# Dense products of a graph-network kernel over 136 instead of 144 columns, on one Trainium2 core

## The chip, the cores and the metric

The kernel runs on one core of one Trainium2 chip (trn2). The metric is device time in microseconds (us) of one execution. A profiled execution gives the trace from which all rows here come. Engines are called PE (TensorE), DVE (VectorE), ACT (ScalarE), POOL (GpSimd) and SP (SyncE, which here only issues transfers).

## What is computed

A graph network of two layers over 6250 nodes and 100000 edges, 128 features each, then a residual sum and a layer norm. The edges are sorted by their target `dst`.

```python
def _layer(h, edge_feats, src, dst, deg, iso, Wn, Ws, Wi, num_nodes):
    msg = (h[src] + edge_feats) @ Wn.T
    agg = jax.ops.segment_sum(msg, dst, num_segments=num_nodes)
    agg = agg / jnp.maximum(deg, 1.0)[:, None]
    self_msg = jnp.where(iso[:, None], h @ Wi.T, h @ Ws.T)
    x = agg + self_msg
    return jnp.where(x >= 0, x, RRELU_SLOPE * x)
...
    h = _layer(x, edge_feats, src, dst, deg, iso, Wn0, Ws0, Wi0, num_nodes)
    h = _layer(h, edge_feats, src, dst, deg, iso, Wn1, Ws1, Wi1, num_nodes)
...
x = _layernorm(x + h)
```

## The kernel before, in words

**Chunks, windows, groups.** 128 edges are a chunk, four chunks a window, four windows a group of 2048 edges. There are 782 real chunks, 196 windows and 49 groups (0 to 48). Since edges are sorted by target, the targets of a window fit in `W` = 40 consecutive columns of `sums`, and those of a group in `SPAN` = 144. The work runs in beats, one window to a beat as a rule.

**Two ways to sum the rows of h.** The way of the windows: POOL gathers, for each chunk, the 128 source rows by an indirect DMA (`gather`, line 511; each row is three bf16 parts of an f32 value), and PE multiplies them by a one-hot matrix of 40 columns into a `ps_win` bank (`sum_chunk`, line 1190), which DVE adds to `sums` (`add_window`, line 731). There are `ROWS` = 5 window slots for gathered rows, so POOL may be at most five gathered windows ahead: it waits on `window_summed`. The dense way: for a group that is kept, DVE makes two one-hot matrices per chunk (`make_codes`, lines 714 to 720), PE multiplies them into a count matrix (`count_piece`, lines 1239 and 1243), ACT writes it from PSUM to `counts` (`keep_chunk`, line 1044). A kept group then has, for each of 49 tiles of 128 nodes, a block of 128 x 144 counts, and `multiply` (line 1251) computes `h_parts` times `counts`: 49 tiles x 3 parts = 147 matmuls of 144 columns a group, all into one PSUM bank. `take_dense` (line 753) adds the bank to 144 columns of `sums`.

**Layer 0.** 31 groups are counted and stored to HBM (`store_counts`); 20 of them (`USED`) are also multiplied by PE in this layer, bank `ps_dense`, in pieces of five or six tiles a beat between the window's matmuls and the count pieces, as `plan_layer0` lays them out. The other groups' rows are gathered: 442 gathers from `x_parts_rows`, after 20 early ones. As a rule two windows of three are gathered; in four steps (with groups 7, 19, 31, 43) one of three. Each trio of 384 nodes whose sums are complete passes through the node stages; its new rows go to `h_parts_rows`.

**Layer 1.** All 31 kept groups are multiplied (`multiply_kept`), their counts loaded back by SP in 217 cuts of seven tiles, 21 cuts ahead. The 18 others (72 windows, 286 gathers from `h_parts_rows`) are gathered. PE does a few cuts and then one window in each beat; the node stages of a trio (lines 1303 and 1316) follow when its sums are complete.

**Setup.** DVE tests in the setup that the input fits the layout (line 616 on), collects the differences side by side in `wrong`, takes their largest (line 636), and the flag `general` made of it (line 681) sends the engines into the fast program or into a slow general one. PE, ACT and POOL start their main work behind that flag.

Of the kernel before, what the change touches and what calls it, by code (L numbers as in the profile page):

```python
# [46 lines left out]
def gnn_resnorm_kernel(nc, x_rows, x_cols, src, dst, edges, wn0, ws0, wi0, wn1, ws1, wi1, out):  # L47
    f32, i32 = mybir.dt.float32, mybir.dt.int32
    bf16, f16 = mybir.dt.bfloat16, mybir.dt.float16
    ALU, ACT, AX = mybir.AluOpType, mybir.ActivationFunctionType, mybir.AxisListType  # L50
# [13 lines left out]
    GC = 16  # L64
    GW = GC // SUB
    GROUPS = CHUNKS // GC
    STEPS = GROUPS // 3
    W = 40
    CW = 13
    UP = 7  # L70
    SPAN = 144
    CLEAN = 24
    PARTS = 3
    CUT = 7
# [5 lines left out]
    BANKS = 3  # L80
# [6 lines left out]
    assert GROUPS == 3 * STEPS + 1 and TRIOS == STEPS + 1 and TILES % CUT == 0  # L87
    assert COLS == TRIOS * TRIO and CHUNKS % GENERAL == 0 and N + P + SPAN <= COLS

# [7 lines left out]
    USED = sorted([g for g in KEPT if g % 3 == 0] + [7, 19, 31, 43])  # L97
# [55 lines left out]
    h_parts_rows = nc.dram_tensor("h_parts_rows", (P + TILES * P, PARTS * D), bf16, kind="Internal").ap()  # L153
    counts_kept = nc.dram_tensor("counts_kept", (len(KEEPABLE), P, TILES * SPAN), bf16, kind="Internal").ap()

# [3 lines left out]
    with ctx:  # L159
        def sb(name, shape, dt=f32):  # L160
            return ctx.enter_context(nc.sbuf_tensor(name, shape, dt))

        def sem(name):
            return ctx.enter_context(nc.semaphore(name))

        SUM, DEG = range(2)
        sums = sb("sums", [P, 2, COLS])
        h_parts = sb("h_parts", [P, TILES, PARTS, D], bf16)
        counts = sb("counts", [P, BUFFERS, TILES, SPAN], bf16)

# [59 lines left out]
        def bank(name, n=1):  # L230
            return ctx.enter_context(nc.psum_tensor(name, [P, n, 512], f32))

        ps_win = [bank(f"ps_win{i}") for i in range(2)]
        ps_count = bank("ps_count", BANKS)
        ps_dense = bank("ps_dense")
# [8 lines left out]
        setup_step = sem("setup_step")  # L244
# [78 lines left out]
        def at(v, n=1):  # L323
            return bass.ds(v, n)
# [16 lines left out]
        def steps(t):  # L341

            return t[:, :].rearrange("p (s c) -> p s c", c=2 * GC)
# [14 lines left out]
        def dense_bank(nth):  # L358

            if nth < len(USED):  # L360
                return ps_dense[:, 0, 0:SPAN]
            return ps_count[:, (nth - len(USED)) % BANKS, 0:SPAN]

        def real(u):

# [11 lines left out]
        def _(sp):  # L377
# [59 lines left out]
            def load_counts(q):  # L437
# [6 lines left out]
                if q >= BUFFERS * CUTS:  # L444
                    sp.wait_ge(cut_multiplied, q - BUFFERS * CUTS + 1)
                t = slice(CUT * cut, CUT * (cut + 1))
                sp.dma_start(counts[:, i % BUFFERS, t, :].rearrange("p t s -> p (t s)"),
                             counts_kept[FIRST_COL[KEPT[i]] // GC, :, CUT * cut * SPAN:CUT * (cut + 1) * SPAN]
                             ).then_inc(counts_loaded[q % (BUFFERS * CUTS)], 16)
# [105 lines left out]
        def _(dve):  # L555
            def setup(ins):
                ins.then_inc(setup_step, 1)
                done[0] += 1
                return done[0]
# [16 lines left out]
            bases = dst_f[0:1, :]  # L576
# [10 lines left out]
            for i in range(CUTS + 1):  # L587
                if i < CUTS:
                    t = slice(CUT * i, CUT * (i + 1))
# [3 lines left out]
                if i:  # L593
                    t = slice(CUT * (i - 1), CUT * i)
# [5 lines left out]
            grouped = bases[:, 0:3 * STEPS * GC].rearrange("p (g c) -> p g c", c=GC)  # L600
# [5 lines left out]
            n = setup(nc.vector.tensor_tensor(stride, bases[:, 1:3 * STEPS * GC + 1], bases[:, 0:3 * STEPS * GC],  # L606
                                              ALU.subtract))
# [3 lines left out]
            def part(count):  # L611
                place[0] += count
                return wrong[:, place[0] - count:place[0]]
# [7 lines left out]
            last = by_group[:, :, GC - 1]  # L621
            setup(nc.vector.tensor_scalar(part(3 * STEPS), last, float(CW - SPAN), None, ALU.add))
            setup(nc.vector.tensor_scalar(part(3 * STEPS), last, -1.0, float(SPAN - CLEAN - CW), ALU.mult, ALU.add))
            firsts = bases.rearrange("p (k c) -> p k c", c=SUB)[:, :, 0]
            ahead = part(WINDOWS)
            n = setup(nc.vector.tensor_tensor(ahead[:, 0:WINDOWS - 1], firsts[:, 1:WINDOWS], firsts[:, 0:WINDOWS - 1],
                                              ALU.subtract))
            n = setup(nc.vector.tensor_scalar(ahead[:, WINDOWS - 1:WINDOWS], firsts[:, WINDOWS - 1:WINDOWS],
                                              -1.0, float(N), ALU.mult, ALU.add))
# [3 lines left out]
            n = setup(nc.vector.tensor_tensor(part(GROUPS), first_dst[:, :],  # L633
                                              bases.rearrange("p (g c) -> p g c", c=GC)[:, :, 0], ALU.subtract))
# [6 lines left out]
            for b in range(2):  # L641
                c = slice(HALF * b, HALF * (b + 1))
# [7 lines left out]
            n = setup(nc.vector.tensor_tensor(below[:, HALF:], dst_f[:, HALF - 1:CHUNKS - 1], ps_count[:, 1, 0:HALF],  # L650
                                              ALU.subtract))
            dve.wait_ge(setup_step, n)
            n = setup(nc.vector.reduce_max(bad[:, 0:1], below[:, 1:], AX.X))
            n = setup(nc.vector.tensor_reduce(rel_w[:, 0:1], above, AX.X, ALU.min))
            dve.wait_ge(setup_step, n)
            n = setup(nc.vector.scalar_tensor_tensor(bad[:, 0:1], rel_w[:, 0:1], -1.0, bad[:, 0:1], ALU.mult, ALU.max))
            dve.wait_ge(setup_step, n)
            n = setup(nc.vector.tensor_tensor(bad[0:1, 0:1], bad[0:1, 0:1], bad[0:1, 1:2], ALU.max))
# [6 lines left out]
            n = setup(nc.vector.tensor_single_scalar(high, src_i, 7, ALU.logical_shift_right))  # L665
            dve.wait_ge(setup_step, n)
            setup(nc.vector.tensor_copy(steps(lane), of_kept(low)))
            n = setup(nc.vector.tensor_copy(tile_of, high))
# [6 lines left out]
            n = setup(nc.vector.scalar_tensor_tensor(steps(before)[:, :, 1:2 * GC], below_now[:, :, 1:2 * GC], float(-P),  # L675
                                                     tile_now[:, :, 0:2 * GC - 1], ALU.mult, ALU.add))
            n = setup(nc.vector.memset(steps(before)[:, :, 0:1], float(P)))
# [45 lines left out]
            def load_columns(table, first, count):  # L723
                return nc.values_load_multi_w_load_instructions(
                    table[0:1, first:first + count], (mybir.EngineType.DVE,), min_val=P, max_val=COLS - SPAN,
                    skip_runtime_bounds_check_because="the setup keeps the bases within the columns")[1]
# [18 lines left out]
            def take_dense(g, windows, added):  # L745

                col = load_columns(base_i, GW * g, 1)[0]
                if windows:
                    dve.wait_ge(window_added, windows)
                if added:  # L750
                    dve.wait_ge(dense_added, added)
                s = sums[:, SUM, at(col, SPAN)]
                nc.vector.tensor_tensor(s, s, dense_bank(added), ALU.add).then_inc(dense_added, 1)  # L753

            def node_inputs(layer, u):
# [243 lines left out]
        def _(act):  # L999
# [25 lines left out]
            def begin_job(j):  # L1025

                b = j % BUFFERS
                if j >= BUFFERS:
                    act.wait_ge(counts_stored[b], 16 * (j // BUFFERS))
                    if JOBS[j - BUFFERS] in USED:  # L1030
                        act.wait_ge(group_multiplied, USED_JOBS.index(j - BUFFERS) + 1)
                end = counts[:, b, :, SPAN - CLEAN:].bitcast(f32)
                nc.scalar.copy(end, zeros[:, 0:CLEAN // 2].unsqueeze(1).to_broadcast([P, TILES, CLEAN // 2]))

# [131 lines left out]
        def _(pe):  # L1166
# [80 lines left out]
            def multiply(b, bank, t0, t1):  # L1247

                for t in range(t0, t1):
                    for k in range(PARTS):  # L1250
                        last = nc.tensor.matmul(bank, h_parts[:, t, k, :], counts[:, b, t, :],  # L1251
                                                start=(t == 0 and k == 0), stop=(t == TILES - 1 and k == PARTS - 1))
                return last

            def multiply_counted(j, t):

                nth = USED_JOBS.index(j)
                if t == 0:
                    pe.wait_ge(piece_kept, 2 * GC * (j + 1))
                    if nth:  # L1260
                        pe.wait_ge(dense_added, nth)
                last = multiply(j % BUFFERS, dense_bank(nth), t, t + 1)
                if t == TILES - 1:
                    last.then_inc(group_multiplied, 1)

            def multiply_kept(q):

                i, cut = divmod(q, CUTS)
                nth = len(USED) + i
                pe.wait_ge(counts_loaded[q % (BUFFERS * CUTS)], 16 * (q // (BUFFERS * CUTS) + 1))  # L1270
                if i == 0:
                    pe.wait_ge(parts_loaded[cut], 16)
                if q == 0:
                    pe.wait_ge(piece_kept, 2 * GC * len(JOBS))
                if cut == 0 and i >= BANKS:
                    pe.wait_ge(dense_added, nth - BANKS + 1)
                multiply(i % BUFFERS, dense_bank(nth), CUT * cut, CUT * (cut + 1)).then_inc(cut_multiplied, 1)
# [184 lines left out]
```

## Time and profile before

| | |
|---|---|
| median of 3 runs | 1088.06 us (1087.48 to 1088.09) |
| the profiled execution, its own time | 1087.0 us |
| its span, first to last instruction | 1085.2 us |
| mean granted clock of TensorE | 0.963 |
| PE busy, share of the span | 954.0 us, 88% |
| POOL busy | 751.6 us, 69% |
| DVE busy | 692.2 us, 64% |
| ACT busy | 514.9 us, 47% |

Setup takes the first 38 us or so, layer 0 runs until about 680 us, a passage between the layers until 707 us, layer 1 from there on. Busy shares are of the whole span and hide that the two layers use the engines differently. Matmuls are pipelined: the duration of one says how long it is under way, and what it costs PE is the distance from its start to the next one's.

### The profile page before, as it was taken

The page shows a single profiled execution, that of the slowest core. Times are in us where ns is not written, and L with a number is a line of the kernel's source. Part 1 is how long each engine was busy: PE and PEld are TensorE (multiplying, and loading weights), DVE is VectorE, ACT ScalarE, POOL GpSimd, SP SyncE. Part 2 cuts the span into 40 slices and gives each one's busy share as a digit, 9 for nine tenths or more (in the row PEclk, how much of TensorE's full clock was granted, in tenths as well). Part 3 has the DMA queues.
Part 4 walks back from the last instruction along what each step waited for, and adds up shares of the span by engine and source line. Part 5 has one row for each costly group of instructions (what it writes and reads, how often), then busy time and mean ns, then how long its engine had stood idle before and what let it go on. Part 6 is the DMA issues. An engine that isn't in the chain of part 4 may idle for free.

```text
span 1085.2 us, 38525 instructions
## 1 busy us (share of the span) xinstructions
PE 954.0 (88%) x14592; PEld 894.2 (82%) x14592; DVE 692.2 (64%) x2386; ACT 514.9 (47%) x1143; POOL 751.6 (69%) x757
## 2 busy tenths in 40 slices
PE   1599999999999998998889987579999999999992
PEld 0489888888888887887878877479999999999991
DVE  8878987888897898887878875312334232423333
ACT  7477777777787787786767774100000000000000
POOL 8467756777767777767777547077777777777772
PEclk9999999999999999999999999589999999999995
DMA  9468878878888787787778768699988898889732
GB/s 306 154 199 275 287 224 277 274 256 274 276 269 276 242 307 248 254 300 257 232 247 283 241 213 306 218 366 312 278 272 269 266 283 264 266 268 286 230 103 69
DMA packets 154041, 277.50 MB, mean 256 GB/s; under 512 B 21458, under 2 KB 112572, under 8 KB 149884
## 3 DMA queue, kind: packets, MB, share of 16 engines
q1 hardware_dynamic: 93504, 184.10, 50.7%
q0 software_dynamic: 35584, 72.92, 23.1%
q10 hardware_dynamic: 24764, 17.95, 5.2%
q8 instruction: 120, 1.97, 0.7%
q14 instruction: 69, 0.57, 0.2%
HBM read 202.58 MB, written 72.30 MB: 253 GB/s over the span
## 4 chain that ended last, share of the span: by engine, by line
PE 46%; issue 5%; POOL 5%; DVE 3%; DMA 3%; ACT 2%; SPq 1%; ACTq 1%; DVEq 0%; POOLq 0%
PE ps_count L1251 24%; PE ps_win L1190 6%; PE ps_dense L1251 6%; POOL rows L511 5%; PE ps_count L1239 4%; PE ps_self L1303 3%; DMA rows<-x_parts_rows,idx 2%; PE ps_node L1316 2%; ACT counts L1044 1%; SPq L434 1%; DMA counts<-counts_kept 1%; DVE is_code L720 1%; DVE is_lane L718 1%; PE ps_win L1197 1%; PE ps_self L1285 1%
## 5 line engine op out<-in xcount | busy, mean ns | idle before, releaser
L511 POOL DMA_INDIRECT rows<-x_parts_rows,idx x442 | 445.8, 1008 | 197.1 <-issue 127.9
L1044 ACT CAST counts<-ps_count 128x294 f32 x992 | 437.7, 504 | 152.4 <-PE ps_count L1239 67.7
L511 POOL DMA_INDIRECT rows<-h_parts_rows,idx x286 | 275.7, 964 | 111.2 <-issue 81.7
L1239 PE MATMUL ps_count<-is_code,is_lane 128*128 128x294 bf16 x992 | 300.5, 309 | 34.4 <-ACT counts L1044 32.4
L1251 PE MATMUL ps_dense<-counts,h_parts 128*128 128x144 bf16 x2940 | 320.7, 227 | 3.4 <-DVE sums L753 3.3
L1251 PE MATMUL ps_count<-counts,h_parts 128*128 128x144 bf16 x4557 | 299.0, 227 | 10.3 <-DMA counts<-counts_kept 10.3
L1251 PEld LDWEIGHTS ps_count<-counts,h_parts 128*128 128x128 bf16 x4557 | 289.9, 98 | 11.1 <-DMA counts<-counts_kept 10.7
L1190 PE MATMUL ps_win<-onehot,feats 128*128 128x40 f32 (+1 forms) x1564 | 244.2, 235 | 20.3 <-DVE sums L731 12.2
L1251 PEld LDWEIGHTS ps_dense<-counts,h_parts 128*128 128x128 bf16 x2940 | 214.5, 98 | 39.0 <-ACT counts L1044 5.0
L1190 PEld LDWEIGHTS ps_win<-onehot,feats 128*128 128x128 f32 (+1 forms) x1564 | 206.7, 158 | 25.1 <-issue 15.7
L720 DVE TENSOR_SCALAR is_code<-codes,code 128x637 bf16<-128x637 f16 x496 | 196.8, 397 | 0.0
L731 DVE TENSOR_TENSOR sums<-sums,ps_win 128x80 f32 (+1 forms) x268 | 59.0, 220 | 182.1 <-PE ps_win L1190 130.2
L1056 ACT COPY self_sums<-ps_self 128x384 f32<-128x384 f32 (+1 forms) x34 | 16.1, 474 | 319.9 <-PE ps_self L1303 319.9
L1190 PE MATMUL ps_win<-onehot,rows 128*128 128x40 bf16 (+1 forms) x2224 | 149.0, 186 | 15.4 <-issue 10.6
L718 DVE TENSOR_SCALAR is_lane<-column,lane 128x128 bf16<-128x128 bf16 x496 | 135.8, 274 | 36.2 <-PE ps_count L1243 34.4
L1190 PEld LDWEIGHTS ps_win<-onehot,rows 128*128 128x128 bf16 (+1 forms) x2224 | 131.3, 112 | 17.1 <-issue 17.1
L1239 PEld LDWEIGHTS ps_count<-is_code,is_lane 128*128 128x128 bf16 x992 | 108.0, 110 | 44.6 <-ACT counts L1044 39.3
L1243 PE MATMUL ps_count<-is_before,is_lane 128*128 128x49 bf16 x465 | 88.5, 190 | 0.0
L690 DVE TENSOR_TENSOR onehot<-column,rel 128x160 f32<-128x160 bf16 x268 | 84.4, 317 | 1.7 <-issue 1.7
L705 DVE TENSOR_TENSOR feats<-feats_rest 128x512 bf16<-128x512 f32 x78 | 58.4, 749 | 2.7
L1190 PE MATMUL ps_win<-onehot,feats_rest 128*128 128x40 bf16 x310 | 56.0, 182 | 0.0
L703 DVE TENSOR_TENSOR feats_rest<-feats 128x512 f32<-128x512 f32 x78 | 53.1, 681 | 3.7 <-DMA feats<-in_edges_dram 3.7
(97 smaller groups left out, 784.2 us busy)
## 6 DMA issues: line engine op xcount, KB each, us to landing
counts_kept<-counts SPq DMA_DIRECT2D x31, 1764.0 KB
counts<-counts_kept SPq DMA_DIRECT2D x217, 252.0 KB, 4.1
feats<-in_edges_dram SPq DMA_DIRECT2D x196, 256.0 KB
rows<-x_parts_rows,idx POOLq DMA_INDIRECT x442
x_parts_rows<-h_parts SPq DMA_DIRECT2D x7, 672.0 KB
h_parts<-h_parts_rows SPq DMA_DIRECT2D x7, 672.0 KB, 9.4
h_parts_rows<-row_parts ACTq DMA_DIRECT2D x16, 288.0 KB
rows<-h_parts_rows,idx POOLq DMA_INDIRECT x286
```

The source lines that it names most:

```text
L511: nc.gpsimd.indirect_dma_start(rows[:, SUB * slot + c, :], None, table[:, :], bass.IndirectOffsetOnAxis(ap=indices[:, c:c + 1], axis=0)).t ...
L690: nc.vector.tensor_tensor(onehot[:, h:h + SUB, :], column[:, 0:W].unsqueeze(1).to_broadcast([P, SUB, W]), rel[:, chunk:chunk + SUB].unsque ...
L703: nc.vector.tensor_tensor(rest, f, upper(f), ALU.subtract).then_inc(feats_rest_made, 1)
L705: nc.vector.tensor_tensor(lower(f), rest, upper(rest), ALU.subtract).then_inc(feats_split, 1)
L718: nc.vector.tensor_scalar(is_lane[:, n % (AHEAD + 1), :], column[:, :], lane[:, col:col + 1], None, ALU.is_equal)
L720: nc.vector.tensor_scalar(is_code[:, n % AHEAD, :], codes[:, :], code[:, col:col + 1], None, ALU.is_equal).then_inc(codes_ready, 1)
L731: return nc.vector.tensor_tensor(s, s, p, ALU.add)
L1044: nc.scalar.copy(counts[:, j % BUFFERS, :, at(offset + first, count)], ps_count[:, q % BANKS, 0:count * TILES].rearrange("p (r t) -> p t r ...
L1190: last = nc.tensor.matmul(ps[:, 0, SUM * w:(SUM + 1) * w], left, right, start=first and i == 0, stop=final and i == len(lefts) - 1)
L1239: last = nc.tensor.matmul(ps[:, 0:count * TILES], is_lane[:, n % (AHEAD + 1), :], is_code[:, n % AHEAD, first * TILES:(first + count) * TI ...
L1243: last = nc.tensor.matmul(ps[:, 0:TILES], is_lane[:, (n - 1) % (AHEAD + 1), :], is_before[:, (n // 4) % 3, n % 4, :], start=False, stop=True)
L1251: last = nc.tensor.matmul(bank, h_parts[:, t, k, :], counts[:, b, t, :], start=(t == 0 and k == 0), stop=(t == TILES - 1 and k == PARTS - 1))
```

## The change

The products of kept groups take columns 0 to 135 of a count block, where they took all 144; their banks and the slice of `sums` that `take_dense` adds to are 136 wide. The blocks themselves, their storing and their loading stay 144 wide. In the setup one more test is made: from the first target of a group to that of the next it must be at most 135. No instruction changes its place in the order of its engine; DVE has two more, and the reduction at line 636 reads 48 more values.

```diff
     SPAN = 144
+    WIDE = 136
...
             if nth < len(USED):
-                return ps_dense[:, 0, 0:SPAN]
-            return ps_count[:, (nth - len(USED)) % BANKS, 0:SPAN]
+                return ps_dense[:, 0, 0:WIDE]
+            return ps_count[:, (nth - len(USED)) % BANKS, 0:WIDE]
...
+            reach = part(3 * STEPS)
+            n = setup(nc.vector.tensor_tensor(reach, bases.rearrange("p (g c) -> p g c", c=GC)[:, 1:3 * STEPS + 1, 0],
+                                              grouped[:, :, 0], ALU.subtract))
+            dve.wait_ge(setup_step, n)
+            setup(nc.vector.tensor_scalar(reach, reach, float(1 - WIDE), None, ALU.add))
...
-                s = sums[:, SUM, at(col, SPAN)]
+                s = sums[:, SUM, at(col, WIDE)]
                 nc.vector.tensor_tensor(s, s, dense_bank(added), ALU.add).then_inc(dense_added, 1)
...
-                        last = nc.tensor.matmul(bank, h_parts[:, t, k, :], counts[:, b, t, :],
+                        last = nc.tensor.matmul(bank, h_parts[:, t, k, :], counts[:, b, t, 0:WIDE],
```

## Rows read from the trace of the kernel before

**Rows 1.** The page, costliest groups: busy us, mean ns | idle before, releaser.

```profile
L511 POOL DMA_INDIRECT rows<-h_parts_rows,idx x286 | 275.7, 964 | 111.2 <-issue 81.7
L1251 PE MATMUL ps_dense<-counts,h_parts 128*128 128x144 bf16 x2940 | 320.7, 227 | 3.4 <-DVE sums L753 3.3
L1251 PE MATMUL ps_count<-counts,h_parts 128*128 128x144 bf16 x4557 | 299.0, 227 | 10.3 <-DMA counts<-counts_kept 10.3
```

**Rows 2.** Stretches: busy us (count) of PE, PEld, DVE, ACT, POOL; clock, DMA share, GB/s.

```profile
200.00:300.00 100.00, 93.32 (x1466) 85.16 (x1464) 86.28 (x301) 76.35 (x177) 76.83 (x77) 1.00 0.83 274
900.00:1000.00 100.00, 99.52 (x1661) 99.10 (x1659) 36.26 (x135) 3.14 (x9) 76.23 (x79) 1.00 0.90 271
```

**Rows 3.** POOL's waits, 700 to 1086 us: us in total, times, longest.

```profile
POOL rows L511 <- issue: 81.7, 268, 0.3
...
POOL rows L511 <- PE ps_win L1190: 5.2, 17, 0.3
```

**Rows 4.** POOL in order of time: start us, us; the last two begin and end layer 1.

```profile
171.59 1.09 POOL L511 DMA_INDIRECT rows<-x_parts_rows,idx  x1 [2.04 <-PE ps_win L1197]
...
327.93 0.94 POOL L511 DMA_INDIRECT rows<-x_parts_rows,idx  x1 [1.96 <-issue]
...
704.62 0.94 POOL L511 DMA_INDIRECT rows<-h_parts_rows,idx  x1 [24.39 <-DMA h_parts_rows<-row_parts]
...
1066.20 0.95 POOL L511 DMA_INDIRECT rows<-h_parts_rows,idx  x1 [0.30 <-issue]
```

**Rows 5.** The chain of waits in layer 1: start us, us, what.

```profile
707.39 5.63 PE ps_count L1251 x63
...
719.88 3.94 PE ps_count L1251 x63
723.83 0.56 issue
...
1058.70 3.43 DMA rows<-h_parts_rows,idx
```

**Rows 6.** The chain of waits in layer 0, 424 to 435 us: start us, us.

```profile
424.69 9.19 DMA rows<-x_parts_rows,idx
...
434.43 0.13 PE ps_count L1239
434.56 0.19 PE ps_dense L1251 x3
434.75 0.14 PE ps_win L1190 x6
```

**Rows 7.** PE's and POOL's longest waits in layer 0, from 60 us on.

```profile
PE ps_count L1239 <- ACT counts L1044: 31.3, 42, 1.9
...
POOL rows L511 <- PE ps_win L1197: 55.9, 38, 7.0
```

**Rows 8.** Line 1251 alone, 60 to 645 us: count, duration, first and last start.

```profile
L1251 PE MATMUL ps_dense<-counts,h_parts x2838: 222/224/328, 62.5 to 644.6; 128*128 128x144 bf16 x190
```

**Rows 9.** Shares of the chain of waits, in 500 to 560 and 560 to 645 us.

```profile
by line: PE ps_dense L1251 18.3%; issue 18.3%; PE ps_count L1239 13.5%; PE ps_win L1190 11.9%; DVE is_code L720 5.5%; DVE is_lane L718 3.9%; ACT counts L1044 2.5%; PE ps_self L1303 2.4%; DVE feats_rest L703 2.0%; DVEq L724 2.0%; DVE row_par
by line: PE ps_dense L1251 27.2%; PE ps_count L1239 20.7%; PE ps_win L1190 17.4%; ACT counts L1044 6.0%; issue 4.8%; PE ps_self L1303 3.3%; ACTq L1020 3.3%; PE ps_self L1285 2.7%; PE ps_win L1197 2.5%; PE ps_count L1243 1.8%; DVEq L724 1.6%
```

**Rows 10.** DVE in the setup, in order of time.

```profile
26.68 0.22 DVE L633 TENSOR_TENSOR counts<-first_dst,counts 1x49 f32<-1x49 f32 x1
26.93 1.56 DVE L636 TENSOR_REDUCE bad<-counts 1x1 f32<-1x1365 f32 x1
...
37.19 0.14 DVE L681 TENSOR_SCALAR general<-ps_node 1x1 int32<-1x1 f32 x1
```

**Rows 11.** Two stretches of lower granted clock (columns as in rows 2), and PE just before the first.

```profile
150.80:154.20 3.40, 3.40 (x36) 3.08 (x34) 2.33 (x11) 1.54 (x4) 0.00 (x0) 0.50 0.76 245
628.70:632.10 3.40, 3.40 (x38) 2.84 (x36) 2.99 (x10) 2.72 (x6) 2.26 (x3) 0.50 0.72 199
149.91 0.32 PE L1239 MATMUL ps_count<-is_code,is_lane 128*128 128x343 bf16 x1 [1.47 <-ACT counts L1044]
```

## The prediction

> **What bounds the kernel now.** I read the groups of instructions first, then busy time by stretches, then POOL's waits, then the chain of waits of each layer. In the groups the products on line 1251 are 7497 matmuls of 144 columns, 2940 in layer 0 and 4557 in layer 1, by far PE's largest item; that they last 227 ns each is their latency, not their cost [rows 1]. By stretches PE looks like the bound of both layers: 93% busy in layer 0 and 99.5% in layer 1 [rows 2]. The reader should not stop there. POOL is 76% busy in both, but a gather keeps it busy for 964 ns and is followed by a gap of 0.3 us [rows 1, 3]. In layer 1 all 285 gaps are of that kind: 268 put down to nothing, 17 to PE, and none, of either sort, longer than 0.3 us [rows 3]. POOL never stands still there. Its first gather starts at 704.62 and its last at 1066.20 us [rows 4]: 361.58 / 285 = 1.269 us for each. Layer 1 is thus as long as 286 gathers, and PE, nearly full, runs beside them. The chain says the same at both ends: at 723.83 us PE, having done 63 products, waits 0.56 us before its next window, and at the end the chain goes through a gather's landing at 1058.70 us [rows 5]. In layer 0 POOL does wait for PE, 55.9 us in all with one wait of 7.0 us, and PE waits for ACT, 31.3 us in 42 waits [rows 7]: PE is the usual bound, with interruptions.
>
> **The price of a column.** In the chain 63 products take 3.94 us, 62.5 ns each, and 3 take 0.19 us [rows 5, 6]. A window's 6 matmuls of 40 columns, with weight loads of the same size, take 0.14 us, 23 ns each, and a count piece of 294 columns 0.13 us [rows 6]. From 40 to 144 columns a column costs (62.5 - 23) / 104 = 0.38 ns, from 144 to 294 it costs (130 - 62.5) / 150 = 0.45 ns. These are the ends; I take 0.417 ns, one column per clock at the higher of the two levels (2.4 GHz), which lies between them. Eight columns are 3.3 ns a matmul (3.0 to 3.6).
>
> **PE's work.** Over both layers 7497 x 3.33 ns = 25.0 us of PE time go, 9.8 in layer 0 and 15.2 in layer 1.
>
> **Layer 1: nothing on the path.** The 15.2 us are hidden by POOL, whose 286 x 1.269 us do not depend on PE: it goes from release to gather with room to spare. PE will stand before its windows for rows, by 15.2 / 72 = 0.2 us a window, and be later for nothing. I take 0; a gain up to 15.2 us is the first rival.
>
> **Layer 0: about half.** Up to 645 us there are 2838 products [rows 8], 2838 x 3.33 ns = 9.5 us over 582 us. After that the chain is POOL's until the layers change, so the last 102 count for nothing. Two deductions. First, gathers bind here too, in places. In a step of twelve beats eight windows are gathered: 32 x 1.269 us = 40.6 us, while twelve beats of PE take 12 x 3.2 = 38.4 us (582 us over the 183 windows that lie there). Only the four steps with a fourth group, of 16 gathers, let POOL catch up. At the end of such a run the chain has a landing of 9.19 us at 424.69 us, after which PE goes on [rows 6]. From POOL's last long pause before it, of 1.96 us until 327.93 us [rows 4], to that landing's end at 433.9 us a faster PE only waits longer: 106 us, or 1.7 us of the 9.5. A run of the same make begins after a wait of 2.04 us at 171.59 us [rows 4] and should end at about 280; no wait of PE shows there, so I give it half, 0.9 us. That leaves 6.9. Second, ACT and DVE: line 1251 has 18.3% of the chain in 500 to 560 us, 11.0 us, and 27.2% in 560 to 645 us, 23.1 us [rows 9]. All its products there, at 2838 x 62.5 ns / 582 = 0.305 us a microsecond, would be 18.3 and 25.9 us. So 34.1 of 44.2 us, 77%, lie on the path. 6.9 x 0.77 = **5.3 us** gained. The ends are 2 us, if PE runs into ACT's evacuation each time, and 10.2 us, all 2838 at 3.6 ns.
>
> **Setup: 0.4 us lost.** DVE works without a pause from the tests to the flag at 37.19 us, and all main work is behind that. The new subtraction and the new addition, over 48 values each, have no row; the nearest is the subtraction over 49 values, 0.22 us, whose successor, which waits for it, starts 0.25 us after it [rows 10]. Two such steps cost at most 0.5 us, and 0.15 us if only their starts count; I take 0.35 us, and for the reduction 48 / 1365 x 1.56 = 0.05 us. Ends: 0.2 and 0.7 us. The addition on line 753 gets shorter by 8 columns, 51 times, beside PE's work: 0. Transfers keep their size: 0. The test itself holds for the reference's inputs: the largest of the 48 distances is 135, the last value allowed.
>
> **The sum.** -5.3 + 0.4 = -4.9 us. The profiled execution took 1087.0 us (its span 1085.2), so it would take 1082.1; the median of the runs is 1.1 us above it, and 1088.06 - 4.9 = **1083.2 us**.
>
> **Rivals.** *PE bounds layer 1 after all* (8%). For it: 99.5% busy. If the gathers got faster as PE takes less, both layers would gain: 9.5 x 0.77 + 15.2 - 0.4 = 22.1, 1066 us; half of it 1077. Against it: 285 gaps without one long wait.
>
> *Gathers and ACT swallow layer 0 too* (11%). If the run from 171 us on is fully bound and what PE gains goes into its 42 waits for ACT, 2 - 0.4 = 1.6 us are left: 1086.5 us, no change that can be told (a measurement of this kernel tells 0.2%, 2.2 us).
>
> *The change saves no PE time* (5%). Weight loads stay 128 columns, and a load is under way in 99.1 of 100 us [rows 2]. If a pair of load and product had a floor near 62 ns, 136 columns would cost the same, and 1088.5 us come out. Against it: pairs of 40 columns follow each other in 23 ns [rows 6], though only in sixes and twelves.
>
> The Trainium skill, "TensorE: Matmul & The Clock Gate", section Back-to-back issue gap, has the spacing in a stream of loads and matmuls set by both, with about 81 ns for 128 columns. By that rule this would be the outcome; but this trace has 62.5 ns for 144 columns in 63 of them, so its figure does not hold here [rows 5].
>
> *The clock falls more often* (6%, slower). Six stretches of 3.4 us in layer 0 have a granted clock of 0.50 (the 1.2 GHz level), the first at 150.80, the last at 628.70 us; just before the first PE had waited 1.47 us for ACT [rows 11]. Less work between equal waits makes PE's idle share larger. A stretch at the lower level costs 5.63 - 3.94 = 1.69 us, by the 63 products that start at 707.39 us against later ones [rows 5]. Six more would cost 10.1 us: 1088.1 - 4.9 + 10.1 = 1093.3 us. It decides from (4.9 + 2.2) / 1.69 = 4.2, so from five more. Against it: in 200 to 300 us, with 7% idle, the clock stays at 1.00 [rows 2].
>
> **How the numbers follow.** The forecast has 70%, and its cases with a gain over 2.2 us some 69; the rivals have 8, 11, 5 and 6. Faster by over 0.2%: 0.69 + 0.08 = 0.77. Within 0.2%: 0.01 + 0.11 + 0.05 = 0.17. Slower: 0.06. The range begins at 1078.3, the median less 10.2 us and with 0.4 us of setup, which leaves out most of the first rival, and ends at 1087.3, which takes in the second rival with the upper bound of the setup and leaves out the two others.
>
> **What would show it.** Right: products of 136 columns 59.2 ns apart in layer 1 (63 in 3.73 us); PE's busy share in 900 to 1000 us down from 99.5% to about 95%, with waits before line 1190; POOL's first and last gather of layer 1 still 361 to 363 us apart; POOL's first gather of layer 1 some 5 us earlier than 704.62; the flag 0.4 us later. Wrong: the distance between the first and last gather shrinks with PE's work (first rival); 63 products still take 3.94 us (third); more than nine stretches at the lower clock in layer 0 (fourth). If the first gather of layer 1 moves by less than 2 us, my share of layer 0 was too large; if by 9, the two deductions were wrong.

## The result

The change is faster by 0.36%: the ratio to the kernel before is 0.9964 with a 95% interval from 0.9951 to 0.9977. The medians of 20 runs each are 1085.21 us (1080.18 to 1087.57) and 1087.88 us (1083.88 to 1093.31). By the ratio that is 1087.88 x 0.0036 = 3.9 us (2.5 to 5.3), where 4.9 us were forecast.

Single executions of this kernel differ by several us, so one pair of profiles doesn't show the gain: the profiled execution after took 1087.57 us, with a span of 1085.8 us against 1085.2. What the profile does show is where time was freed and what stood in its place.

The page and its groups, the counterpart of [rows 1]. PE's busy time fell from 954.0 to 933.4 us:

```profile
PE 933.4 (86%) x14592; PEld 869.7 (80%) x14592; DVE 691.7 (64%) x2388; ACT 513.5 (47%) x1143; POOL 760.0 (70%) x757
...
L512 POOL DMA_INDIRECT rows<-h_parts_rows,idx x286 | 278.1, 972 | 111.9 <-issue 84.8
...
L1258 PE MATMUL ps_dense<-counts,h_parts 128*128 128x136 bf16 x2940 | 311.0, 224 | 3.9 <-DVE sums L760 2.2
L1258 PE MATMUL ps_count<-counts,h_parts 128*128 128x136 bf16 x4557 | 282.1, 223 | 10.0 <-DMA counts<-counts_kept 10.0
```

The chain of waits of layer 1 after (start us, us, what), as in [rows 5]: 63 products in 3.73 us, 59.2 ns each, where it was 3.94 us.

```profile
713.35 3.73 PE ps_count L1258 x63
718.30 3.73 PE ps_count L1258 x63
```

The same two stretches as in [rows 2], same columns. PE's share in layer 1 went from 99.52 to 94.46%, in layer 0 from 93.32 to 91.61%, and the DMA's in layer 1 from 0.90 to 0.88; DVE, ACT and POOL moved by half a point at most.

```profile
200.00:300.00 100.00, 91.61 (x1454) 83.29 (x1450) 86.28 (x303) 76.22 (x178) 76.83 (x77) 1.00 0.83 276
900.00:1000.00 100.00, 94.46 (x1636) 93.20 (x1634) 35.77 (x134) 3.14 (x9) 76.21 (x79) 1.00 0.88 270
```

Waits in 700 to 1086 us (us in total, times, longest): first PE before a window, before the change, then the same after it, then POOL after.

```profile
PE ps_win L1190 <- issue: 10.6, 9, 2.7
...
PE ps_win L1190 <- DMA rows<-h_parts_rows,idx: 4.7, 1, 4.7
```

```profile
PE ps_win L1197 <- issue: 29.6, 24, 3.9
```

```profile
POOL rows L512 <- issue: 84.8, 278, 0.3
POOL rows L512 <- DMA h_parts_rows<-row_parts: 25.0, 1, 25.0
POOL rows L512 <- PE ps_win L1197: 2.1, 7, 0.3
```

That is the story of layer 1. PE stood 10.6 + 4.7 = 15.3 us before its windows and now stands 29.6 us, 14.3 more for 15.2 us of work less, and POOL still has no gap over 0.3 us. A wait "for issue" is one for which the trace shows no releaser; before a window it is most likely for the landing of gathered rows. POOL's first and last gather of layer 1 after, against [rows 4]:

```profile
703.13 0.94 POOL L512 DMA_INDIRECT rows<-h_parts_rows,idx  x1 [25.02 <-DMA h_parts_rows<-row_parts]
...
1067.15 0.95 POOL L512 DMA_INDIRECT rows<-h_parts_rows,idx  x1 [0.30 <-issue]
```

They are 364.0 us apart, 1.277 us a gather, where it was 361.6 and 1.269. That is a little over the 361 to 363 us that I had named, and not for the 136 columns: the same distance is 361.7 us in a run with 136 columns in layer 1, and 364.4 us in the one with 144 there, 136 in layer 0 and half of that layer's gathers (both below).

The new test in the setup, DVE in order of time, against [rows 10]; the first fence is an earlier instruction in the trace before, whose counterpart begins the second:

```profile
24.88 0.41 DVE L618 TENSOR_SCALAR counts<-counts 1x512 f32<-1x512 f32 x1
```

```profile
25.40 0.41 DVE L619 TENSOR_SCALAR counts<-counts 1x512 f32<-1x512 f32 x1
...
26.29 0.22 DVE L627 TENSOR_TENSOR counts<-counts 1x48 f32<-1x48 f32 x1
26.55 0.18 DVE L630 TENSOR_SCALAR counts<-counts 1x48 f32<-1x48 f32 x1
26.65 0.50 DVE L633 TENSOR_TENSOR counts<-counts 1x195 f32<-1x195 f32 x1
...
27.68 1.61 DVE L643 TENSOR_REDUCE bad<-counts 1x1 f32<-1x1413 f32 x1
...
37.99 0.15 DVE L688 TENSOR_SCALAR general<-ps_node 1x1 int32<-1x1 f32 x1
```

From the start of the subtraction to that of the next old instruction it is 26.65 - 26.29 = 0.36 us, and the reduction takes 0.05 us more: 0.41 us. The flag itself came 0.80 us later than before (37.99 against 37.19), but 0.52 us of that was there before the first new instruction (25.40 against 24.88); from there to the flag it is 12.59 us against 12.31, 0.28 us more.

### The profile page after: what moved, and what is told of

The parts are those of the page before. It is cut to its first block, busy times and chain, and to the rows that moved or that the text cites. A ratio compares the mean times of both kernels' runs of the same rounds, so it can differ in the third digit from the quotient of the medians.

```text
span 1085.8 us, 38527 instructions
## 1 busy us (share of the span) xinstructions
PE 933.4 (86%) x14592; PEld 869.7 (80%) x14592; DVE 691.7 (64%) x2388; ACT 513.5 (47%) x1143; POOL 760.0 (70%) x757
## 4 chain that ended last, share of the span: by engine, by line
PE 48%; issue 6%; DVE 4%; DMA 3%; ACT 2%; POOL 2%; ACTq 1%; DVEq 0%; SPq 0%; POOLq 0%
PE ps_count L1258 25%; PE ps_win L1197 7%; PE ps_dense L1258 6%; PE ps_count L1246 5%; PE ps_self L1310 3%; PE ps_node L1323 2%; POOL rows L512 2%; DMA rows<-x_parts_rows,idx 1%; ACT counts L1051 1%; DVE is_code L727 1%; DMA counts<-counts_kept 1%; PE ps_win L1204 1%; DMA h_parts_rows<-row_parts 1%; DVE is_lane L725 1%; PE ps_self L1292 0%
## 5 line engine op out<-in xcount | busy, mean ns | idle before, releaser
L512 POOL DMA_INDIRECT rows<-x_parts_rows,idx x442 | 450.9, 1020 | 189.0 <-issue 127.9
L1258 PE MATMUL ps_dense<-counts,h_parts 128*128 128x136 bf16 x2940 | 311.0, 224 | 3.9 <-DVE sums L760 2.2
L1258 PE MATMUL ps_count<-counts,h_parts 128*128 128x136 bf16 x4557 | 282.1, 223 | 10.0 <-DMA counts<-counts_kept 10.0
L1258 PEld LDWEIGHTS ps_count<-counts,h_parts 128*128 128x128 bf16 x4557 | 273.5, 98 | 10.7 <-DMA counts<-counts_kept 10.4
L1258 PEld LDWEIGHTS ps_dense<-counts,h_parts 128*128 128x128 bf16 x2940 | 210.2, 98 | 39.7 <-ACT counts L1051 5.1
L1197 PEld LDWEIGHTS ps_win<-onehot,feats 128*128 128x128 f32 (+1 forms) x1564 | 205.9, 158 | 28.1 <-issue 19.9
L1197 PE MATMUL ps_win<-onehot,rows 128*128 128x40 bf16 (+1 forms) x2224 | 149.0, 186 | 32.4 <-issue 29.6
```

What stands on the lines that cost most here:

```text
L512: nc.gpsimd.indirect_dma_start(rows[:, SUB * slot + c, :], None, table[:, :], bass.IndirectOffsetOnAxis(ap=indices[:, c:c + 1], axis=0)).t ...
L1197: last = nc.tensor.matmul(ps[:, 0, SUM * w:(SUM + 1) * w], left, right, start=first and i == 0, stop=final and i == len(lefts) - 1)
```

## The experiments

The theory: layer 1 is as long as POOL's gathers, so what PE saves there is lost; in layer 0 PE bounds, but not everywhere, so about half counts. Rivals: PE's time counts alike in both layers; products don't get cheaper. Each ratio is to the kernel before, run beside it on the same chip, with its 95% interval; where us are given for a ratio, they are the ratio times 1088.

**One layer at a time.** The width of bank, slice and product is set by layer, `WIDE0` and `WIDE1`.

```diff
+    WIDE0, WIDE1 = 136, 144
...
-                        last = nc.tensor.matmul(bank, h_parts[:, t, k, :], counts[:, b, t, 0:WIDE],
+                        last = nc.tensor.matmul(bank, h_parts[:, t, k, :], counts[:, b, t, 0:bank.shape[-1]],
```

> 136 columns in layer 0 alone, 144 in layer 1, with the new test. Gathers bound layer 1 (my theory): all of the change's gain stands, 3.9 us (ratio 0.996). Rival, PE's time counts alike in both layers: 2940 of 7497 products, so 1.5 us (0.9986). Either way the first gather of layer 1 to the last takes 361 to 365 us.

> 136 columns in layer 1 alone, 144 in layer 0, with the new test. My theory: no gain, -0.5 to +1 us (1.000), products 59.2 ns apart, PE's busy share from 900 to 1000 us down to about 95% and gathers of layer 1 as before, 1.27 us each. Rival (PE counts in both layers): 2.4 us faster (0.9978).

Layer 0 alone: 0.9954 (0.9928 to 0.998), 5.0 us. Layer 1 alone: 1.0007 (0.9981 to 1.0032), nothing. The second run's POOL in order of time, and its stretch of 900 to 1000 us with the columns of [rows 2]:

```profile
710.57 0.94 POOL L513 DMA_INDIRECT rows<-h_parts_rows,idx  x1 [25.19 <-DMA h_parts_rows<-row_parts]
...
1072.29 0.94 POOL L513 DMA_INDIRECT rows<-h_parts_rows,idx  x1 [0.30 <-issue]
```

```profile
900.00:1000.00 100.00, 96.40 (x1674) 95.45 (x1672) 34.27 (x131) 3.14 (x9) 75.93 (x79) 1.00 0.87 268
```

361.7 us from first to last gather, within 0.2 us what it was, with PE relieved of 15 us. The whole gain is layer 0's. For the first run alone the rival's 1.5 us lie outside the interval of 2.2 to 7.8 us; for the second its 2.4 us lie just outside that of -3.5 to +2.1 (negative is slower), so the ratios of this pair alone lean to the theory and the trace settles it.

**A cut large enough to see.** `WIDE0, WIDE1 = 96, 96`: a product over 96 columns, columns 96 to 143 left out.

> Products and sums over 96 columns in both layers; leaves out the columns 96 to 143 of each group's product. A product should cost 96 x 0.417 + 2.5 = 42.5 ns, so that PE is relieved of 20 ns x 2940 = 59 us in layer 0 and 91 us in layer 1. My theory: layer 1 keeps its length (first to last gather 361 to 365 us) and layer 0 gives back 15 to 35 us, until gathers and ACT bind: 1053 to 1073 us. Rival (PE bounds layer 1): about 960 us. Third (a floor for a pair of weight load and product near 60 ns): 1084 us.

0.9865 (0.9806 to 0.9923), 14.7 us of 150 us of PE time, from a median of 1073.26 us. Its chain of waits, a stretch of layer 1, and POOL's first and last gather there:

```profile
726.78 2.68 PE ps_count L1259 x63
```

```profile
900.00:1000.00 100.00, 79.09 (x1622) 77.46 (x1619) 34.05 (x125) 2.93 (x8) 75.92 (x80) 0.93 0.86 269
```

```profile
685.83 0.95 POOL L513 DMA_INDIRECT rows<-h_parts_rows,idx  x1 [23.91 <-DMA h_parts_rows<-row_parts]
...
1049.45 0.95 POOL L513 DMA_INDIRECT rows<-h_parts_rows,idx  x1 [0.30 <-issue]
```

2.68 / 63 = 42.5 ns, as 96 x 0.417 + 2.5 gives: no floor for a pair of load and product down to there. PE is 79% busy in layer 1, and the gathers still take 363.6 us. Layer 0 gave back less than expected: 14.7 us, just under the 15 to 35. In this execution the granted clock also fell more often in layer 0: 47.8 us at 0.50 up to 650 us, where it was 20.5 before. PE's row up to 650 us (busy, clock, DMA share, GB/s), before and here:

```profile
0.00:650.00 650.00, 567.22 (x8416) 0.98 0.79 257
```

```profile
0.00:650.00 650.00, 551.64 (x8713) 0.96 0.81 265
```

By the prediction's price of 1.69 us for a stretch of 3.4 us, the 27.3 us more at the lower clock are some 13.5 us of PE time, an estimate.

**Gathers of layer 1 made fewer.** Three gathers of four; a quarter of that layer's gathered rows is left out.

```diff
+        def gathers_in(n):
+
+            return min(chunks_in(n), 3) if n >= WINDOWS else chunks_in(n)
...
-                    gather((x_parts_rows, h_parts_rows)[layer], idx[:, chunk:chunk + SUB], r % ROWS, chunks_in(n))
+                    gather((x_parts_rows, h_parts_rows)[layer], idx[:, chunk:chunk + SUB], r % ROWS, gathers_in(n))
```

> The kernel before (144 columns) with three gathers of four in each window of layer 1; the fourth chunk's products use what its slot last held, so a quarter of layer 1's gathered rows are left out. POOL's work there falls to 216 x 1.27 = 273 us, PE's stays. My theory: PE now bounds layer 1, at 99.5% of 362 less some 15 us of waits, so the time is 10 to 16 us under that of the kernel before (0.985 to 0.991), and PE's products follow without waits before windows. Rival (PE bounded layer 1 all along): no change, 1.000.

> The same with the change (136 columns). My theory: with PE as the bound the 15.2 us of layer 1 show, and layer 0 gives its 4: 17 to 21 us under the run with 144 columns and as few gathers, some 30 us under the kernel before (0.972). Rival (the products were never worth 3.3 ns each in time, for whatever reason): 4 us under the other.

144 columns: 0.9864 (0.9831 to 0.9897). 136 columns: 0.9715 (0.9686 to 0.9745). The pair differs by 0.0149, 16.2 us, give or take 5 (medians 1074.67 and 1055.65, 19.0 us), where 17 to 21 was expected and with all gathers it is 3.9. The same edit is now worth four times as much, because PE has become layer 1's bound. PE's stretch, POOL's waits in 710 to 1060 us and line 1255's starts with 144 columns:

```profile
900.00:1000.00 100.00, 100.00 (x1674) 99.89 (x1672) 36.02 (x134) 3.14 (x9) 58.45 (x62) 1.00 0.87 255
```

```profile
POOL rows L515 <- PE ps_win L1194: 82.7, 56, 3.5
POOL rows L515 <- issue: 52.8, 158, 3.3
```

```profile
L1255 PE MATMUL ps_count<-counts,h_parts x4557: 222/226/328, 713.0 to 1052.2; 128*128 128x144 bf16 x199
```

and with 136, where the line is 1262:

```profile
L1262 PE MATMUL ps_count<-counts,h_parts x4557: 219/223/321, 703.5 to 1028.4; 128*128 128x136 bf16 x199
```

From first to last product 339.2 and 324.9 us: 14.3 us, against 15.2 by the price of a column. And with 144 columns POOL waits for PE, 82.7 us, where in this layer no wait put down to PE was over 0.3 us before. This also shows what a real wait of POOL looks like in that view: a longest wait of 3.5 us, not 0.3. The name in the row doesn't tell, for waits up to 3.3 us stand under "issue" here; the length does.

**Gathers of layer 0 made fewer.** Two of four after the first five windows; PE uses the second chunk's rows for the third and fourth, so half of layer 0's gathered rows are left out.

```diff
+            return min(chunks_in(n), 2) if n < WINDOWS and n not in GATHERED[:RAW] else chunks_in(n)
...
-                last = sum_chunk(layer, ps_win[n % 2], SUB * (r % ROWS) + c, SUB * (n % FEATS) + c,
+                last = sum_chunk(layer, ps_win[n % 2], SUB * (r % ROWS) + min(c, gathers_in(n) - 1), SUB * (n % FEATS) + c,
```

> The kernel before with two gathers of four in each window of layer 0 (after the first five); PE uses the second chunk's rows for the third and fourth, so half of layer 0's gathered rows are left out. POOL can bind nothing in layer 0. What it shows is how much gathers cost layer 0 before: my theory, 3 to 8 us, mostly at its end, where the last gathers and their landing are in the chain (1080 to 1086 us). Rival (PE and ACT alone set layer 0): under 1.5 us.

> The same with 96 columns in layer 0 (columns 96 to 143 left out) and 144 in layer 1. With all gathers, 96 columns shortened layer 0 by 17 to 18 us of PE's 57. If gathers took the rest (my first deduction), this run is 40 us or more under the run with 144 columns and half the gathers. If ACT and DVE took it (my second), it is 15 to 20 us under it. Most likely between, 30 us.

> 136 columns in layer 0, 144 in layer 1, and two gathers of four in each window of layer 0 (the third and fourth chunk use the second's rows). Against the run with 144 columns and as few gathers (0.9955 of the kernel before): if gathers took 2.6 us of the 9.5 and ACT and DVE the rest of what was lost, as forecast, 7.3 us less, 0.989; if gathers took nothing, 4.4 us less, 0.9915. With 96 columns the pair differed by 23 us for 57 us of PE, which in proportion would be 3.8 us, 0.992.

| layer 0 | all gathers | half of them |
|---|---|---|
| 144 columns | 1 | 0.9955 (0.993 to 0.998), 4.9 us |
| 136 columns | 0.9954 (0.9928 to 0.998), 5.0 us | 0.9895 (0.9868 to 0.9921), 11.4 us |
| 96 columns | 0.9865 (0.9806 to 0.9923), 14.7 us | 0.9742 (0.9712 to 0.9772), 28.1 us |

(The 96 of the first column has 96 columns in layer 1 too, which there is worth nothing.) With half the gathers, 136 columns give 11.4 - 4.9 = 6.5 us, give or take 4, and 96 columns 23.2 us. That is 1.5 to 2.6 us more than with all gathers for 136 columns (the 6.5 against 5.0 or 3.9) and 8.5 us more for 96, and neither shows what gathers hold back. The first difference is smaller than its uncertainty. The second is 8.5 us, give or take 8, and the clock can account for all of it: up to its last product in layer 0, at 634.4 us, the run with 96 columns and half the gathers had 23.9 us at 0.50, the one with all gathers 47.8, some 12 us of PE time by the price above. The larger part of what 96 columns save is lost with half the gathers too, 57 - 23 = 34 us. There PE's waits in 60 to 645 us are:

```profile
PE ps_count L1251 <- ACT counts L1056: 37.8, 51, 2.2
PE ps_win L1202 <- DVE sums L743: 15.9, 13, 2.4
```

The waits for ACT rose from 31.3 to 37.8 us and those for DVE from 8.0 to 15.9 us, in a layer that is 30 us shorter. DVE is 87% busy there. That is 14.4 of the 34 us. The clock takes at most 2 more (23.9 us at 0.50 against 20.5). The rest shows in no row of waits. That ACT and DVE take it too is likely and not shown; no run relieved them.

**A use for PE's room.** PE has 5% free in layer 1 and POOL none, so work should go from POOL to PE. Group 40 is left out of the kept groups (16 gathers); here it is kept.

```diff
-    KEPT = [g for g in KEEPABLE if g not in (40,)]
+    KEPT = [g for g in KEEPABLE if g not in ()]
```

> The change, with group 40 kept too: 16 gathers of layer 1 less, 147 products of layer 1 and 16 chunks of counting in layer 0 more. My theory: POOL has 270 x 1.27 = 343 us of work in layer 1, PE 0.955 x 362 + 147 x 0.0592 - 1 = 353 us, so layer 1 is 8 us shorter and PE's; layer 0 grows by 16 x 0.29 = 4 to 5 us where PE bounds it: 3 to 4 us faster than the change, 7 faster than before (0.993). Rival (PE already bounds layer 1): 8 + 4 us slower than the change, 8 slower than before.

1.0046 (1.0019 to 1.0073): 5 us slower than before, a miss. Layer 1 did get shorter, 343.1 us of gathers where 363 to 364 were, even more than expected. But the last gather of layer 0 came at 704.76 us, not 677 to 680: with group 40 the plan of layer 0 has beats with one chunk or none to count, for want of a counts buffer (14 of 188, none before), and beats with four to make up for it (33, where it had 5). So the plan's numbers were changed with it, at both widths.

```diff
-    JOBS, BUILDS, MULTIPLIED, BUILT_BEAT, DONE_BEAT = plan_layer0(KEPT, USED, 188, BUFFERS, GC, TILES, 5.6, 8)
+    JOBS, BUILDS, MULTIPLIED, BUILT_BEAT, DONE_BEAT = plan_layer0(KEPT, USED, 188, BUFFERS, GC, TILES, 6.2, 6)
```

> The change with group 40 kept, as before, and the plan of layer 0 with 6.2 tiles a beat (it was 5.6) and a head of 6 chunks (8), so that no beat is left without counting for want of a buffer. Layer 1 should stay 18 us shorter than the change's (343 us of gathers). If the 27 us by which layer 0 had grown came from the stalled plan, it grows by 5 to 12 us now and the time is 6 to 13 us under the change's (0.985 to 0.991 of the kernel before). If ACT's 14 us and DVE's of 16 more chunks set it, it is as the first trial was, 1.00.

> The same with 144 columns. With group 40 kept, PE has 31 x 147 + 147 = 4704 products in layer 1: 345 + 9.2 - 1 = 353 us of work against 343 us of gathers, so PE bounds layer 1 and the change's 15.7 us should show in part: 10 us in layer 1 and 4 in layer 0, 12 to 15 us over the run with 136. Rival (layer 1 stays the gathers'): 4 us over it.

136 columns: 0.9965 (0.9945 to 0.9985), the change's own 0.9964, where 0.985 to 0.991 was expected. 144 columns: 1.0162 (1.0135 to 1.0189). The two differ by 0.0197, 21 us, for the same 8 columns, where 12 to 15 was expected. In 900 to 1000 us PE is full again with 136 columns; line 1258 there and line 1251 with 144 columns show that the products of layer 1 run for 333.4 and 349.0 us:

```profile
900.00:1000.00 100.00, 100.00 (x1731) 99.88 (x1729) 35.07 (x133) 3.44 (x10) 76.21 (x79) 1.00 0.90 282
```

```profile
L1258 PE MATMUL ps_count<-counts,h_parts x4704: 219/223/321, 723.7 to 1057.1; 128*128 128x136 bf16 x196
```

```profile
L1251 PE MATMUL ps_count<-counts,h_parts x4704: 222/226/328, 727.7 to 1076.7; 128*128 128x144 bf16 x196
```

15.6 us, where 4704 x 3.33 ns = 15.7: with this split every column counts in the products of layer 1. With 136 columns its gathers are 21 us shorter than the change's, but layer 0 grew by nearly as much: its last gather came at 694.81 us, 17.7 us later. With 144 columns it came at 700.02 us, where it was 679.28, 684.43 and 684.39 in the three traces with 144 columns and all gathers, 17.3 us later than their mean. The other plan numbers took 10 us off the first trial's 27.6; what is left goes with 16 more chunks to count, 1.1 us each. I had put their cost at 0.3 us. No version here beats the change.

## Why the prediction was right

Faster was forecast by 4.9 us, measured are 3.9 (2.5 to 5.3), so the forecast lies within the interval. That layer 1 gives nothing and layer 0 gives all is shown; the size of layer 0's gain is confirmed, while its two deductions were not confirmed one by one. Point by point:

- *The price of a column*, 3.33 ns for eight: 63 products went from 3.94 to 3.73 us, 3.33 ns each. 42.5 ns at 96 columns fit the same line. The rival of a floor for a pair of load and product falls with it. The figure of some 81 ns for 128 columns in the Trainium skill, "TensorE: Matmul & The Clock Gate", section Back-to-back issue gap, is not what a stream of such pairs took here: 62.5 ns at 144 columns and 42.5 ns at 96, with 128 itself not run.
- *Layer 1: nothing on the path.* Shown four ways: no gain with layer 1 alone; gathers that take 361.7 and 363.6 us with 15 and 91 us less work on PE; a gain of 16 us once a quarter of the gathers is gone; POOL's waits. The first rival, PE as the bound, is refuted. PE's share of 94.5% in 900 to 1000 us and the waits before line 1197 came as said. A third candidate, the transfers themselves, was not tested by a run; against it, POOL issues 77 gathers in 100 us of layer 0 at a DMA share of 0.83 and 79 in layer 1 at 0.90.
- *Layer 0: 5.3 us of 9.5.* The change's 3.9 us and the setup's 0.4 make 4.3 us, layer 0 alone 5.0 + 0.4. Of the two deductions, gathers were put at 2.6 us (1.7 and 0.9); the runs give 1.5 to 2.6, with an uncertainty of 4, so that nothing at all would fit too. The 77% would make 7.3 us with half the gathers; measured 6.5, give or take 4. How the 4.2 us forecast as lost divide between gathers and ACT and DVE stays open. Taking the share of the chain for the share that counts was good for a small cut. For a large one it isn't: with 96 columns 23 of 57 us counted, 41%.
- *Setup: 0.4 us.* 0.41 us by the instructions added, 0.28 us on the way to the flag in the pair. The sign that I had named, a flag 0.4 us later, was 0.80 us, and is too coarse for this: in the nine kept traces with the test the flag comes at 37.09 to 38.91 us, on average 37.73, in the four without it at 37.43. The upper bound of 0.7 us was also too wide by its own terms, which give 0.5 + 0.05 us; even with 0.7 us the second rival ends at 1086.8 us, not at the 1087.3 at which the range was closed.
- *POOL's first gather of layer 1 some 5 us earlier.* In the pair of profiles it is 1.5 us earlier, less than the 2 us under which I had called my share of layer 0 too large. That test was badly set: single executions vary by more. With 144 columns and all gathers in layer 0 it came at 704.62, 710.57 and 710.00 us, with 136 at 703.13, 704.32 and 701.09: on average 5.5 us earlier.
- *The clock falls more often.* 27.3 us at 0.50 up to 650 us of the profiled execution, where it was 20.5, and as much in the run with layer 0 alone. But it is 34.1 us in the run with 136 columns in layer 1 alone, which has 144 in layer 0. Over the eight traces with the old plan and 136 or 144 columns in layer 0 it is 17.1 to 27.3 us with 136, on average 23.1, and 20.5 to 34.1 us with 144, on average 24.8. So eight columns less don't make it fall more often. In the one trace with 96 columns and all gathers it did (47.8 us).
- *After 645 us nothing counts.* Not tested by itself. Halving the gathers of layer 0 at 144 columns gave 4.9 us. So gathers did hold layer 0 back somewhere, within the 3 to 8 us expected; the interval from 2.2 to 7.6 us lies above the 1.5 us of the case in which PE and ACT alone set it. Where they did is not shown: in its trace layer 0's last gather came at 674.96 us, 4.3 us earlier than before, but layer 1's first at 704.43, only 0.2 us earlier.

## What to carry to other kernels

An engine at 99.5% need not be the bound: look for one whose idle time is all of one small, constant length. POOL's gaps of 0.3 us between gathers were part of its work here, and at 76% busy it was full. Two engines that finish together hide each other: a cut to either is worth nothing until the other gets less work, and a single small move of work (here one group of 49, with the plan fitted to it) changes what the same eight columns are worth from 4 to 21 us. Ask where the freed time can go before making the cut, and judge a change of 0.4% by many runs of both kernels, never by one pair of profiles.

## What was unexpected

Counting one more chunk in layer 0 cost 1.1 us of time (17.7 us for 16 chunks), though PE, ACT and DVE were at 92, 76 and 86% busy there in 200 to 300 us. That is four times PE's own 0.29 us for a chunk and about what ACT needs for it, 992 evictions of 504 ns for 496 chunks, 1.0 us each. Which engine sets it was not tested. Of a large cut to PE alone only 41% showed. And the clock of TensorE fell to 0.50 again and again in layer 1 of the run with 96 columns (mean 0.93 in 900 to 1000 us, PE 79% busy), without making that layer longer.
